# GpSimd multiplies half of the scan's states by C in every second round, from a copy that ScalarE makes

## The reference

```python
def step(state, xs):
    d_t, B_t, C_t, u_t = xs
    dA = jnp.exp(d_t[..., None] * A)
    state = state * dA + (d_t * u_t)[..., None] * B_t[:, None, :]
    y_t = jnp.einsum('ben,bn->be', state, C_t)
    return (state, y_t)
...
y = y + D[None, :, None] * u
y = y * jax.nn.silu(z)
```

## Time and profile before

| what | value |
|---|---|
| time, median of 3 runs (lowest, highest) | 1127.36 us (1126.22, 1128.6) |
| time of the profiled execution | 1126.31 us |
| its span, first to last instruction | 1123.8 us |
| the scan's loop, first scan to `gated(1)` | 49.0 to 186.2 us |
| mean granted TensorE clock of the span, as a share of 2.4 GHz | 0.940 |

### The profile page before, as it was taken

One profiled execution on the slowest core, in us unless ns is written; L12 is line 12 of the kernel. 1 busy time (PEld: TensorE's weight loads), 2 busy tenths in 40 slices (PEclk: granted clock), 3 DMA queues, 4 the chain that ended last, 5 costly groups with the idle time before them and its releaser, 6 DMA issues.

```text
span 1123.8 us, 15428 instructions
## 1 busy us (share of the span) xinstructions
PE 952.9 (85%) x5407; PEld 771.4 (69%) x5407; DVE 777.7 (69%) x1325; ACT 643.4 (57%) x1237; POOL 505.8 (45%) x476
## 2 busy tenths in 40 slices
PE   5277766576999998999788999879989999899898
PEld 1032222245899997899666878767878788688787
DVE  6899998875777776676455555676655756577565
ACT  5857644673777775677534666525656544344443
POOL 0366531214666664665333344434344544254352
PEclk8599789887999999999989999999999999899999
DMA  9201000013000000000080000000000500000000
GB/s 308 94 1 56 0 1 0 1 34 132 1 1 1 2 1 1 1 1 1 1 374 1 1 1 1 1 1 1 1 1 1 210 1 1 1 1 1 20 1 19
DMA packets 4560, 35.91 MB, mean 32 GB/s; under 512 B 1021, under 2 KB 2149, under 8 KB 3109
## 3 DMA queue, kind: packets, MB, share of 16 engines
q1 hardware_dynamic: 4485, 34.93, 8.1%
HBM read 33.88 MB, written 1.05 MB: 31 GB/s over the span
## 4 chain that ended last, share of the span: by engine, by line
PE 49%; DVE 19%; issue 7%; ACT 7%; POOL 2%; ACTq 0%; DVEq 0%; POOLq 0%
PE psum L387 13%; PE psum L389 13%; PE psum L388 13%; DVE f_h_lo L1641 4%; PE psum L628 2%; ACT f_silu L1108 2%; DVE f_silu L1624 2%; PE psum L579 2%; DVE x_norm L1150 2%; DVE f_silu L1633 1%; PE psum L710 1%; PE psum L745 1%; ACT L1108 1%; PE psum L588 1%; DVE a_PT_lo L1445 1%
## 5 line engine op out<-in xcount | busy, mean ns | idle before, releaser
L1633 DVE TENSOR_TENSOR f_silu<-f_silu,psum 128x512 f32<-128x512 f32 x100 | 68.7, 687 | 165.9 <-ACT f_silu L1108 165.9
L387 PE MATMUL psum<-x_norm_T_hi,f_wgu_hi 128*128 128x512 f32 x400 | 177.2, 443 | 0.0
L792 ACT ACTIVATE f_h_hi<-f_silu 128x512 fp32r<-128x512 f32 x100 | 63.0, 630 | 173.6 <-DVE f_silu L1624 173.1
L389 PE MATMUL psum<-x_norm_T_hi,f_wgu_lo 128*128 128x512 f32 x400 | 160.5, 401 | 0.0
L388 PE MATMUL psum<-x_norm_T_lo,f_wgu_hi 128*128 128x512 f32 x400 | 160.2, 400 | 0.0
L387 PE MATMUL psum<-f_wd_hi,f_h_hi 128*128 128x256 f32 x400 | 121.6, 304 | 14.5 <-DVE f_h_lo L1641 14.4
L1641 DVE TENSOR_TENSOR f_h_lo<-f_silu,f_h_hi 128x512 fp32r<-128x512 f32 x100 | 123.7, 1237 | 3.6 <-ACT f_h_hi L792 3.5
L388 PE MATMUL psum<-f_wd_lo,f_h_hi 128*128 128x256 f32 x400 | 114.0, 285 | 0.0
L389 PE MATMUL psum<-f_wd_hi,f_h_lo 128*128 128x256 f32 x400 | 113.9, 285 | 0.0
L1789 POOL TENSOR_TENSOR m_dBu<-m_du,m_Bs 128x1024 f32<-128x1024 f32 x32 | 76.2, 2382 | 77.1 <-DVE m_du L1245 24.7
L1714 POOL TENSOR_TENSOR f_wgu_lo<-f_w,f_wgu_hi 128x512 fp32r<-128x512 f32 x44 | 56.6, 1287 | 103.6 <-ACT f_wgu_hi L792 103.4
(11 more groups left out here) (299 smaller groups left out, 2674.3 us busy)
## 6 DMA issues: line engine op xcount, KB each, us to landing
f_wb<-in_f1b SPq DMA_DIRECT2D x1, 6912.0 KB, 19.3
f_w<-in_f3w SPq DMA_DIRECT2D x1, 5376.0 KB, 16.0
f_wa<-in_f1a SPq DMA_DIRECT2D x1, 3840.0 KB, 13.2
w_raw<-in_w0raw SPq DMA_DIRECT2D x1, 3072.0 KB, 19.4
f_w<-in_f2w SPq DMA_DIRECT2D x1, 3072.0 KB, 25.5
a_wo<-in_wo SPq DMA_DIRECT2D x2, 1024.0 KB, 13.2
a_wq<-in_wq SPq DMA_DIRECT2D x1, 2048.0 KB, 27.1
x_res<-in_x SPq DMA_DIRECT2D x1, 1024.0 KB, 10.3
```

The costliest lines, as they stand in the source:

```text
L387: mm(out, wh, xh, start=start, stop=False, **kw)
L389: return mm(out, wl, xh, start=False, stop=stop, **kw)
L792: return A(out_, in_, ACT.Copy)
L1633: V.tensor_tensor(sg[g % 2][:, :], sg[g % 2][:, :], ps[:, 3 + 2 * (g % 2), :], ALU.mult).then_inc(S("f_m"), 1)
```

## The change

`hst` and `hC` get a third buffer each (the tiles `dA[0]` and `dA[1]`, free in the loop). With it scan `g` waits for product `g - 3` and the sum goes one iteration later on TensorE. In the even rounds 2, 4, ... 30 VectorE multiplies only channel half 0 with C. ScalarE copies bank 3 to `Cs` after VectorE's product of that round (`copy_C`), and GpSimd multiplies half 1 with `Cs` (`hc_half`), after `dBu` of three rounds later. C of the next round waits for that copy, since it overwrites bank 3. What hangs on the sums (`gated(0)` and the work behind it) moves one round later, and so do the last eight value products.

```diff
-    hst = [hst0, zinv]
+    hst = [hst0, zinv, dA[0]]
+    hC.append(dA[1])
+    Cs = spl[:, 1, :]
...
+    POOL_HC = [g for g in range(1, 2 * NS) if g % 2 == 0]
+    def pool_hc(g):
+        return sum(1 for r in POOL_HC if r < g)
-    VALUE_AT = [2 * v for v in range(HEADS // 2)] + [NS + 6 + v for v in range(HEADS // 2)]
+    VALUE_AT = [2 * v for v in range(HEADS // 2)] + [NS + 7 + v for v in range(HEADS // 2)]
...
-            for g in range(2 * NS + 1):
+            for g in range(2 * NS + 2):
                 if g + 3 < 2 * NS:
                     broadcast_B(g + 3)
-                if g:
-                    pe.wait_ge(S("m_hC"), g)
                 if g < 2 * NS:
+                    if g:
+                        pe.wait_ge(S("m_hC"), g)
+                    if pool_hc(g):
+                        pe.wait_ge(S("m_Ccopy"), pool_hc(g))
                     mm(ps[:, 3, :], sel_bc[:, NS + g % NS, :], bcs[g // NS][:, :], start=True, stop=True).then_inc(S("m_C"), 1)
-                if g:
-                    if g == NS + 1:
+                if g >= 2:
+                    if g == NS + 2:
                         pe.wait_ge(S("m_y_read"), 1)
+                    pe.wait_ge(S("m_hC"), g - 1)
+                    if pool_hc(g - 1):
+                        pe.wait_ge(S("m_hCp"), pool_hc(g - 1))
                     for e in range(2):
-                        last = mm(ps[:, e, :], ident[:, :], hC[(g - 1) % 2][:, e, :], start=(g - 1) % NS == 0, stop=(g - 1) % NS == NS - 1)
+                        last = mm(ps[:, e, :], ident[:, :], hC[(g - 2) % 3][:, e, :], start=(g - 2) % NS == 0, stop=(g - 2) % NS == NS - 1)
...
+            def copy_C(g):
+                act.wait_ge(S("m_hC"), g + 1)
+                if pool_hc(g):
+                    act.wait_ge(S("m_hCp"), pool_hc(g))
+                copy(Cs[:, :], ps[:, 3, :]).then_inc(S("m_Ccopy"), 1)
...
+                if g - 2 in POOL_HC:
+                    copy_C(g - 2)
                 if g - 2 in VALUE_AT:
...
+            copy_C(2 * NS - 2)
...
                     dve.wait_ge(S("m_dBu"), g + 1)
-                    if g >= 2:
-                        dve.wait_ge(S("m_hC"), g - 1)
+                    if g >= 3:
+                        dve.wait_ge(S("m_hC"), g - 2)
+                        if pool_hc(g - 2):
+                            dve.wait_ge(S("m_hCp"), pool_hc(g - 2))
...
-                    if g >= 3:
-                        dve.wait_ge(S("m_y"), g - 2)
-                    V.tensor_tensor(hC[(g - 1) % 2][:, :, :], hst[(g - 1) % 2][:, :, :], bc(ps[:, 3, :].unsqueeze(1), [P, 2, HALF]),
-                                    ALU.mult).then_inc(S("m_hC"), 1)
+                    if g >= 4:
+                        dve.wait_ge(S("m_y"), g - 3)
+                    if g - 1 in POOL_HC:
+                        V.tensor_tensor(hC[(g - 1) % 3][:, 0, :], hst[(g - 1) % 3][:, 0, :], ps[:, 3, :], ALU.mult).then_inc(S("m_hC"), 1)
+                    else:
+                        V.tensor_tensor(hC[(g - 1) % 3][:, :, :], hst[(g - 1) % 3][:, :, :], bc(ps[:, 3, :].unsqueeze(1), [P, 2, HALF]),
+                                        ALU.mult).then_inc(S("m_hC"), 1)
...
+                def hc_half(g):
+                    pool.wait_ge(S("m_Ccopy"), pool_hc(g) + 1)
+                    pool.wait_ge(S("m_h"), 2 * (g + 1))
+                    if g >= 3:
+                        pool.wait_ge(S("m_y"), g - 2)
+                    G.tensor_tensor(hC[g % 3][:, 1, :], hst[g % 3][:, 1, :], Cs[:, :], ALU.mult).then_inc(S("m_hCp"), 1)
...
+                    if g - 3 in POOL_HC:
+                        hc_half(g - 3)
+                    if g == 2 * NS - 1:
+                        hc_half(2 * NS - 2)
```

More of the change, by code:

```diff
@@ L457, in ssm @@
                     mm(ps[:, 5, 256:259], ones[:, :], wabs[:, 0:3], start=True, stop=True).then_inc(S("wabs_sum"), 1)
-                if g == NS + 2:
+                if g == NS + 3:
                     pe.wait_ge(S("wvo_copied"), HEADS // 2)
@@ L914, in ssm @@
                     round_weights(ROUND_AT.index(g))
+            copy_C(2 * NS - 2)
+            act.wait_ge(S("wvo_psum"), HEADS)
+            copy(wvo[:, HEADS - 1, :], ps[:, 4 + (HEADS - 1) % 2, 0:DM]).then_inc(S("wvo_copied"), 1)
             quantised_inputs(0)
@@ L1285, in ssm @@
                     dve.wait_ge(S("m_dBu"), g + 1)
-                    if g >= 2:
-                        dve.wait_ge(S("m_hC"), g - 1)
+                    if g >= 3:
+                        dve.wait_ge(S("m_hC"), g - 2)
+                        if pool_hc(g - 2):
+                            dve.wait_ge(S("m_hCp"), pool_hc(g - 2))
                     for e in range(2):
                         dve.wait_ge(S("m_dA"), 2 * g + e + 1)
-                        V.tensor_tensor_scan(hst[g % 2][:, e, :], ps[:, 6 + e, :], dBu[g % 2][:, e, :], 0.0, ALU.mult, ALU.add).then_inc(S("m_h"), 1)
+                        V.tensor_tensor_scan(hst[g % 3][:, e, :], ps[:, 6 + e, :], dBu[g % 2][:, e, :], 0.0, ALU.mult, ALU.add).then_inc(S("m_h"), 1)
                 if g:
@@ L1293, in ssm @@
                     dve.wait_ge(S("m_C"), g)
-                    if g >= 3:
-                        dve.wait_ge(S("m_y"), g - 2)
-                    V.tensor_tensor(hC[(g - 1) % 2][:, :, :], hst[(g - 1) % 2][:, :, :], bc(ps[:, 3, :].unsqueeze(1), [P, 2, HALF]),
-                                    ALU.mult).then_inc(S("m_hC"), 1)
+                    if g >= 4:
[5 more added lines that the diff above has]
+                                        ALU.mult).then_inc(S("m_hC"), 1)
                 if g == 6:
                     quantise_weights()
-                if g == NS + 1:
+                if g == NS + 2:
                     gated(0)
-                if g == NS + 4:
+                if g == NS + 5:
                     dve.wait_ge(S("m_out"), 1)
@@ L1305, in ssm @@
                     V.tensor_copy(scratch[:, 12:13], epsc[:, :]).then_inc(S("m_res"), 1)
-                if g == NS + 5:
+                if g == NS + 6:
                     stats(0)
-                if g == NS + 8:
+                if g == NS + 9:
                     normalise(0, xn[0])
-                if g == NS + 9:
+                if g == NS + 10:
                     dve.wait_ge(S("ln_done"), ln_index[("F0", 0)])
@@ L1790, in _ @@
                                     ALU.mult).then_inc(S("m_dBu"), 1)
-                    if g == NS + 7:
+                    if g - 3 in POOL_HC:
+                        hc_half(g - 3)
+                    if g == 2 * NS - 1:
+                        hc_half(2 * NS - 2)
+                    if g == NS + 8:
                         rstd_of()
```

## The result

| | before | after |
|---|---|---|
| median of 13 runs each (lowest, highest) | 1127.9 us (1126.22, 1130.76) | 1133.02 us (1128.79, 1135.44) |
| profiled execution: time, span | 1126.31, 1123.8 us | 1134.27, 1132.5 us |
| start of `gated(1)` | 186.2 us | 192.2 us |

The changed kernel is slower: the ratio is 1.004 (95% interval 1.0026 to 1.0054), 5.1 us between the medians. The prediction said no change, 1127.0 us, with a range up to 1131.5; the result lies above it, on the side of the rival "slower by the clock" (1131 us).

What follows compares the result with a forecast made beforehand. VectorE was taken to bound the loop, busy for 128.4 of 137.2 us. The terms, -7.6 - 3.7 + 4.6 + 3.3 + 0.7 + 1.7 + 0.7 = -0.3 us, gave 1127.0 us from the median, range 1122.5 to 1131.5.

Steps and rivals of the forecast that it cites:

- slower by the clock: Rival, 22%: in the loop, one more stretch of 10.2 us at 1.2 GHz costs 4 us: 1131 us.
- the ring: Loop over TensorE and ScalarE closed by C waiting for the copy: 7.02 us a pair of rounds, against 6.23 for VectorE.
- GpSimd and the shared ports: Rival, 8%: VectorE's passes in the loop wait for GpSimd's half products, or GpSimd leads: 1130 us.
- (1): Fifteen VectorE products in the loop shrink from 1024 to 512 elements: 7.6 us less.
- (2): With the third buffer no scan waits for the instruction ahead, 22 places of 0.17 us: 3.7 us less.
- (3): Copies of C: 3.2 us of new waits in rounds 9 to 17, 1.4 for rounds 5 to 9, together 4.6.
- (4): Rounds 18 to 25: waits at `gated(0)`, the first output's transposes and the value products, 3.3 us more.
- (5): The loop's end: last product 0.7 us later, and one more sum before `gated(1)`, 1.7 us more.
- (6): Loop start: TensorE's clock rises to 2.4 GHz a round later, with the first sum: 0.7 us more.
- (7): GpSimd's 15 half products in the loop: nothing paid, hidden by its idle time; cover 0.1 us where VectorE leads.
- the row: Quantising pass over `w_raw`: 2.58 us in the loop with GpSimd busy, 1.22 alone; held to speak against the change.

Runs made afterwards that it cites:

- e1: The changed kernel without the copies of C and GpSimd's half products, third buffers and later sum kept: 1124.74 us, 0.9982 of the kernel before.
- e3b: The changed kernel with C copied ahead of VectorE's half product, so the next C waits for the product alone: 1125.77 us, 0.9978 of the kernel before.
- e4: The kernel before with a third buffer for the states alone: 1124.67 us, 0.9978 of the kernel before.
- x1: The changed kernel with the products of rounds 22 and 24 whole on VectorE: 1132.51 us, 1.0048 of the kernel before.
- w2: The changed kernel with products of zeros on TensorE between B and C: 1129.21 us, 1.0011 of the kernel before.
- w1: The kernel before with products of zeros on TensorE between B and C: 1127.09 us, 0.9987 of the kernel before.
- w3: The changed kernel with C copied ahead of the half product and rounds 22 and 24 whole on VectorE: 1122.88 us, 0.9961 of the kernel before.
- x2: The changed kernel with the early copy of C, rounds 22 and 24 whole on VectorE, and zero products on TensorE: 1122.39 us, 0.996 of before.

## Why the prediction was wrong, step by step

The theory after the result was: the tie from the copy to C, and not the half products, makes the kernel slower, in part by the ring and in part by the clock. Its rivals were GpSimd and the shared ports, and the later sum. The later sum is out: e1 has it and is fast. The ports aren't out: they are 2 us of VectorE's other work in the profile, but e3b keeps them whole and is faster than before, so they aren't what turned the gain into a loss. The tie is: e3b takes it away, keeps the rest, and gives back 7.3 us.

- **(1) and (2), less work on VectorE: right.** -10.8 us in the profile against -11.3; e4 gives 3.8 us for (2) by itself (forecast 3.7).
- **(3) the ring: right in place and size.** Where no fall meets them, second scans of rounds 11 to 17 wait 0.5 to 0.6 us; pairs are 6.92 and 7.16 us in turn, 7.20 with zero products. In x1 the waits of rounds 9 to 17 come to 3.1 us, forecast 3.2. With e3b the ring is open and a pair is 6.51.
- **(4) and (5), the second token half and the end: near.** The waits at 131.5 us (2.37, behind the transposes) and at 149.2 (1.65, the value products) were forecast at 1.7 and 3.0. From the last product to `gated(1)` it is 5.60 us as forecast; the last product waits 1.90 us, forecast 1.2.
- **(6) the clock: the step that failed.** It was priced at +0.7 us, for a rise that comes a round later. That part came true: the wait of the first rounds is at 63.96 us and 1.46 us long (0.90). What was missing is that the tie gathers TensorE's idle time into waits of about 2 us for the copy in rounds at full pace, and that the clock falls there too: in three profiles of three with the tie and without zero products, and in none of five without it (the stretches under e3b). The next wait of this kind stands one round later:

```profile
69.84 1.22 DVE L1315 TENSOR_TENSOR_SCAN m_dA<-psum,m_dBu 128x512 f32<-128x512 f32 x1 [2.39 <-ACT psum L918]
```

  It follows the stretch 64.8 to 68.2. With the one behind the stretch of 102.3 (1.62) these are 4.0 us of waits, where w2 and x1, with no fall at these places, wait 0.72 and 0.60. So term (6) was sized at 0.7 us and measured about 3.3: 0.6 for the rise and 2.7 for the two falls. All waits came to +12.2 us against 9.3 forecast (4.6 + 3.3 + 0.7 + 0.7). Keeping TensorE busy takes the changed kernel's waits from 15.9 to 10.0 and 3.0 of the 5.1 us between the medians (w1, w2).
- **(7) GpSimd at nothing: right for scans, wrong for the other passes, and the second step that failed.** Scan `g` + 3 never waits for a half product. The other work of VectorE grew by 2.2 us, nearly as much as the error of the waits (2.9), although the prediction itself said that the row spoke against the change here: 1.5 at the normalising pass, 0.5 at the first quantising pass, 0.2 elsewhere. The Trainium skill, "SBUF — State Buffer", section "SBUF: two separate sides", which gives the two engines one pair of ports with the loser waiting, was right for this, and "pays nothing" held for scans and products: scans stay at 1.21 to 1.22 us.

The loop came out 6.1 us longer, forecast 0.3 shorter. The 6.4 us between are, within rounding, 2.9 of waits, 2.2 of other work, 0.9 of scans (two take 2.26 us together, and 2.36 where the second waits) and 0.5 of products that saved less.

The rival "slower by the clock" had the right direction and cause, and priced it as one more stretch of 10 us in rounds that run at TensorE's pace, 4 us. What came were short stretches of 3.4 us, each of which cost 1.5 to 2 us: 1.5 us for that at 102.3 (x1's two pairs beside it), and 1.7 for that at 64.8 (2.39 against 0.72 in w2). The rule that I set beside it, from the Trainium skill's "TensorE: Matmul & The Clock Gate", section "A second HAM failure mode: psum-queue depth-cycling", that small idle times between groups of products make the clock swing, agrees with those falls. The argument that I held against it, that the same rounds stood at 2.4 GHz with TensorE busy for 70%, was taken from a kernel whose idle time there comes in pieces of at most 1.2 us.

**Open.** What stands behind the loop took 940.3 us after and 937.6 before in the profiles, 937.8 in e1 and 942.5 in e3b, with the same instructions. In the changed kernel the 17.1 us from 201.3, 9.1 us behind `gated(1)`, stand at 1.2 GHz; the kernel before at the same distance from `gated(1)`:

```profile
195.30:212.40 17.10, 8.35 (x44) 4.57 (x45) 16.00 (x36) 6.09 (x7) 1.91 (x1) 0.70 0.01 1
```

There the mean clock is 0.70. But this stretch doesn't order the kernels: e3b has 0.70 too and takes 942.5 us, e4 has 0.51 and takes 940.7. One profile of each kernel doesn't tell how much of the difference of the medians belongs here. Of the 2.1 us that are left between w2 and w1, 2.6 stand at `gated(1)` of the profiles (though w1's profiled execution was its slowest, and longer than w2's); they come from the ring, the later sum and the ports together, and weren't taken apart. A copy of C with a second bank for it was not tried.

## What to carry to other kernels

A copy that takes over an operand frees its bank only when it has run. Put it ahead of the other reader, not behind it: at the end of another engine's queue it closes a ring over all engines (e3b against the changed kernel: 7.3 us for moving the copy). Cost such a ring first as a period against the pace of the leading engine, and then with the slow clock, because idle time on TensorE came back as clock here (3.0 of the 5.1 us between the kernels went when zero products filled it) and, in these profiles, the falls in the paced rounds followed the longer waits. Try the smallest part of a change alone: one more state buffer (e4) gives 3.2 us; the best kernels here, w3 and x2, with all parts in their better places, give 5.3 and 5.1 (1128.21 - 1122.88, 1127.53 - 1122.39).

## What the runs showed of the hardware that was not expected

- Four instructions of VectorE (the normalising pass) took 4.09 us instead of 2.61 when a half product of 1.3 us followed GpSimd's `dBu` at once; one pass of 1.22 us ended 1.1 us behind `dBu` whenever it started, so that shortening the instruction ahead of it saved nothing there.
- Products of zeros, which add work to TensorE, made a kernel faster: 3.8 us where it stood idle for the copy, 1.1 us before the change.
- The same instructions behind the loop varied by up to 5 us between the profiles of the kernels here (937.6 to 942.8 us), with stretches at 1.2 GHz at other places.
